# Attention stage: side work between uses, value and output tiles by twos in a bank, projections copied once, turned maxima copied by VectorE

## The reference

```
qkv = layernorm(x) @ Wqkv + bqkv              # 16 heads of 16 channels
scores = q k^T / 4 - slope[h] * |i - j|       # 1024 x 1024 for each batch element and head
out = softmax(scores) @ v                     # over all 1024 keys, no causal mask
x = x + out @ Wout + bout
```

## Time and profile before

| | us |
|---|---|
| median of 3 runs (3257.17 to 3265.41) | 3258.13 |
| the profiled execution, own time | 3271.27 |
| its span in the trace | 3269.5 |
| first to last score matmul of attention (L1742) | 1248.7 to 2917.9 |
| PE, DVE, ACT, POOL busy over the span | 94%, 78%, 61%, 33% |

### The profile page before, as it was taken

How to read it: one execution, slowest core, us unless ns; L and a number is a source line. 1 busy time by engine, 2 the same in 40 slices (tenths; PEclk the granted TensorE clock), 3 DMA queues, 4 the chain that set the end, 5 groups by cost and what they waited for, 6 DMA issues and landing times. The chain is left out here.

```text
span 3269.5 us, 73440 instructions
## 1 busy us (share of the span) xinstructions
PE 3085.7 (94%) x28196; PEld 1827.7 (56%) x28196; DVE 2534.6 (78%) x5875; ACT 1985.8 (61%) x2967; POOL 1094.2 (33%) x1364
## 2 busy tenths in 40 slices
PE   7999999995999869999999999999999999988999
PEld 3666666664788734444454444444544445437888
DVE  6677877764788658888888889788888887927887
ACT  2455444441666515777777777767777777775665
POOL 3354554443223221332423333323233232222222
PEclk8899999985999958999999999999999999998999
DMA  1000000002111151324232323232322322202111
GB/s 54 2 28 28 28 28 28 20 10 73 66 59 59 39 108 36 58 39 83 40 67 55 57 63 60 43 77 52 71 48 49 74 49 53 57 18 93 52 60 38
DMA packets 126461, 165.34 MB, mean 51 GB/s; under 512 B 23584, under 2 KB 104240, under 8 KB 125456
## 3 DMA queue, kind: packets, MB, share of 16 engines
q1 hardware_dynamic: 115688, 149.37, 18.7%
q0 software_dynamic: 9984, 10.38, 2.4%
q10 hardware_dynamic: 440, 0.90, 0.1%
HBM read 81.58 MB, written 38.24 MB: 37 GB/s over the span
## 5 line engine op out<-in xcount | busy, mean ns | idle before, releaser
L1855 ACT ACTIVATE b_p_t<-banks 128x1024 f32<-128x1024 f32 x1024 | 1040.2, 1027 | 304.0 <-PE banks L1742 238.7
L1681 PE MATMUL banks<-b_k_stack,b_q_stack 62*128 62x512 f32 x2048 | 809.6, 475 | 26.5 <-issue 10.8
L1742 PE MATMUL banks<-b_q_stack,b_k_stack 64*128 64x512 f32 x2048 | 767.8, 450 | 9.9 <-ACT b_p_t L1855 9.9
L1941 DVE CUSTOM_DVE_ANT_1 banks<-banks,b_near_rows 128x512 f32<-128x512 f32 x960 | 649.0, 715 | 138.3 <-PE banks L1681 135.1
L1944 DVE TENSOR_REDUCE b_half_max<-banks 128x1 f32<-128x512 f32 x1024 | 657.8, 684 | 79.9 <-PE banks L1681 76.3
L1696 PE MATMUL banks<-b_p_t,b_v 128*17 128x256 f32 x8192 | 631.8, 386 | 6.3 <-POOL b_p_t L2100 5.5
L1742 PEld LDWEIGHTS banks<-b_q_stack,b_k_stack 64*128 64x128 f32 x2048 | 313.7, 185 | 389.1 <-issue 325.5
L2100 POOL TENSOR_TENSOR b_p_t<-b_p_t,b_fall 128x256 f32<-128x256 f32 x384 | 280.5, 733 | 658.6 <-ACT b_p_t L1855 657.8
L1681 PEld LDWEIGHTS banks<-b_k_stack,b_q_stack 62*128 62x128 f32 x2048 | 341.9, 188 | 111.6 <-DVE b_half_max L1941 35.9
L1696 PEld LDWEIGHTS banks<-b_p_t,b_v 128*17 128x17 f32 x8192 | 142.8, 95 | 300.7 <-issue 162.2
L1148 ACT ACTIVATE ffn_relu<-banks,ffn_scale_fc 128x512 f32<-128x512 f32 x256 | 176.2, 688 | 205.5 <-PE banks L1080 205.5
(11 more groups left out here) (255 smaller groups left out, 5333.6 us busy)
## 6 DMA issues: line engine op xcount, KB each, us to landing
ffn_x<-x SPq DMA_DIRECT2D x32, 512.0 KB, 3.9
b_q_stack<-b_qk_hi SPq DMA_DIRECT2D x252, 64.0 KB
b_k_stack<-b_qk_hi SPq DMA_DIRECT2D x252, 64.0 KB
b_fall<-c_fall SPq DMA_DIRECT2D x48, 256.0 KB, 2.6
a_x<-hidden_states SPq DMA_DIRECT2D x16, 512.0 KB, 3.9
x<-a_x SPq DMA_DIRECT2D x16, 512.0 KB, 2.9
x<-ffn_x SPq DMA_DIRECT2D x16, 512.0 KB, 2.8
b_x<-x SPq DMA_DIRECT2D x8, 1024.0 KB, 5.6
```

Source lines behind the costliest of these rows:

```text
L1681: pe.matmul(m, q_stack[rows, slot, qb * P:(qb + 1) * P], k_stack[rows, slot, half * BANK:(half + 1) * BANK], start=True, stop=True, tile_p ...
L1742: last = pe.matmul(out, k_stack[stack, slot, kb * P:(kb + 1) * P], q_stack[stack, slot, half * BANK:(half + 1) * BANK], start=True, stop=n ...
L1855: act.activation(p_t[use % P_BUFS][:, :, :], scores[use % 2], ACT.Exp, scale=slopes()[pair][0]).then_inc(p_made, 1)
L1941: dve.tensor_tensor_reduce(out=m, in0=m, in1=near_window(pair, qb, rg), scale=1.0, scalar=LOWEST, op0=ALU.add, op1=ALU.max, accum_out=larg ...
```

## The change

- The merge goes by whole uses: `attend` yields once a use instead of twice, so that side work no longer stands between the two halves of one.
- Stacks count eight steps instead of two of weight three, and the halves are made in steps 2 and 3 of them; SP's DMAs stay behind three such steps. ACT copies a half once, as `qk`, and POOL rounds that to `qk_hi` itself before it makes `qk_lo`.
- Value and output tiles go by twos in a bank: one copy of 128x512 where there were two of 128x256. `att_hi`, `att_lo` and `y` have one buffer for two tiles in place of two buffers for one, and the first output step only turns.
- The turned maxima come two maxima later (`TURN` 4) and behind the use's matmuls, and DVE copies them.

```diff
-        STEPS, STACKS, VALUES, NORMALIZE = GROUP * HALVES * QB, 2, QB, 1 + QB
+        STEPS, STACKS, VALUES, NORMALIZE = GROUP * HALVES * QB, 8, QB // 2, 1 + QB
+        STACK_STEPS = {2: 0, 3: 1}
-        LEAD, TURN = 16, 2
+        LEAD, TURN = 16, 4
...
-                side_by_side(*([(STEPS, attend(g, rows), 1)] if g >= 0 else []),
+                side_by_side(*([(STEPS // ROWGROUPS, attend(g, rows), 1)] if g >= 0 else []),
...
-                             *([(STACKS, stacks(g + 2), 3)] if 0 <= g + 2 < ALL else []),
+                             *([(STACKS, stacks(g + 2), 1)] if 0 <= g + 2 < ALL else []),
...
# PE, find_maxima
-                    if g and turn == TURN:
-                        m, (used, n) = misc.take(("turn", g - 1), (shift_copied, g))
...
                         yield
+                    if g and turn == TURN - 1:
+                        m, (used, n) = misc.take(("turn", g - 1), (shift_copied, g))
...
# ACT, make_stacks
-                    act.activation(qk_hi[:, cols], m, ACT.Identity, bias=b_scaled[:, hg:hg + 1],
-                                   scale=scale_qk[:, 0:1]).then_inc(qk_hi_made, 1)
...
# POOL, make_stacks
+                        pool.tensor_copy(qk_hi[:, cols], qk[:, cols]).then_inc(qk_hi_made, 1)
+                        pool.wait_ge(qk_hi_made, use + 1)
                         pool.tensor_tensor(qk_lo[:, cols], qk[:, cols], qk_hi[:, cols].bitcast(F32), ALU.subtract).then_inc(qk_lo_made, 1)
...
# ACT, find_maxima, and DVE, find_maxima
-                        act.activation(shift_full[:, :], m, ACT.Copy, scale=-1.0).then_inc(shift_copied, 1)
+                    if g and turn == TURN:
+                        dve.wait_ge(max_turned, g)
...
+                        dve.tensor_scalar(shift_full[:, :], misc.at["turn", g - 1][0:2 * GROUP * QB, 0:P], -1.0, None, ALU.mult).then_inc(shift_copied, 1)
...
# SP, make_stacks
-                yield
-                yield
+                for _ in range(max(STACK_STEPS)):
+                    yield
                 sp.wait_ge(bias_cast, 16)
                 sp.wait_ge(qk_hi_made, 2 * (g + 1))
                 sp.wait_ge(qk_lo_made, 2 * (g + 1))
```

More of the change, by code:

```diff
@@ L1657, in make_stacks @@
                 pe.wait_ge(x_lo_made, 4 * (b + 1))
-                for half in range(HALVES):
+                for step in range(STACKS):
+                    if step not in STACK_STEPS:
+                        yield
+                        continue
+                    half = STACK_STEPS[step]
                     cols = slice(half * BANK, (half + 1) * BANK)
@@ L1713, in conclude @@
                 pe.wait_ge(att_made, use + 1)
[L1714 to L1717, removed]
+                for n in range(TWOS + 1):
+                    tiles = TWOS * b + n
+                    if n:
+                        m, (used, value) = misc.take(("y", b, n - 1), (y_made, tiles))
+                        pe.wait_ge(used, value)
+                        pe.wait_ge(att_lo_made, tiles)
+                        if tiles == 1:
+                            pe.wait_ge(weights_split, 3)
+                        for j in range(2):
+                            tokens = slice(j * P, (j + 1) * P)
+                            last = in_three(m[:, j * DIM:(j + 1) * DIM], lambda part, kt: (att_hi, att_lo)[part][:, kt, tokens],
+                                            lambda part, kt: w_out[part][:, kt, :])
+                        last.then_inc(y_ready, 1)
+                    if n < TWOS:
+                        m, (used, value) = misc.take(("att", b, n), (att_lo_made, tiles + 1))
+                        pe.wait_ge(used, value)
                         for kt in range(KT):
-                            last = pe.transpose(m[:, kt * P:(kt + 1) * P], att[:, i, kt * P:(kt + 1) * P], ident[:, :])
+                            for j in range(2):
+                                last = pe.transpose(m[:, (kt * 2 + j) * P:(kt * 2 + j + 1) * P], att[:, 2 * n + j, kt * P:(kt + 1) * P], ident[:, :])
                         last.then_inc(att_turned, 1)
[L1721 to L1729, removed]
                     yield
@@ L1828, in conclude @@
                     return
[L1829 to L1843, removed]
+                for n in range(TWOS + 1):
+                    tiles = TWOS * b + n
+                    if n:
+                        act.wait_ge(y_ready, tiles)
+                        if tiles >= 2:
+                            act.wait_ge(y_added, tiles - 1)
+                        act.activation(y[:, :, :], misc.at["y", b, n - 1].rearrange("p (t n) -> p t n", t=2), ACT.Copy).then_inc(y_made, 1)
+                    if n < TWOS:
+                        act.wait_ge(att_turned, tiles + 1)
+                        if tiles:
+                            act.wait_ge(y_ready, tiles)
+                        act.activation(att_hi[:, :, :], misc.at["att", b, n].rearrange("p (k n) -> p k n", k=KT), ACT.Copy).then_inc(att_hi_made, 1)
                     yield
@@ L1966, in conclude @@
                     return
[L1967 to L1976, removed]
+                for n in range(TWOS + 1):
+                    tiles = TWOS * b + n
+                    if n < TWOS:
+                        dve.wait_ge(att_hi_made, tiles + 1)
+                        if tiles:
+                            dve.wait_ge(y_ready, tiles)
+                        dve.tensor_tensor(att_lo[:, :, :], misc.at["att", b, n].rearrange("p (k n) -> p k n", k=KT),
+                                          att_hi[:, :, :].bitcast(F32), ALU.subtract).then_inc(att_lo_made, 1)
                     yield
@@ L2084, in conclude @@
                     return
-                for i in range(QB):
-                    x, tile = xs[b % X_BUFS][:, i, :], QB * b + i
-                    pool.wait_ge(y_made, tile + 1)
-                    pool.wait_ge(x_biased, tile + 1)
-                    pool.tensor_tensor(x, x, y[tile % 2][:, :], ALU.add).then_inc(y_added, 1)
+                for n in range(TWOS + 1):
+                    if n:
+                        x, tiles = xs[b % X_BUFS][:, 2 * n - 2:2 * n, :], TWOS * b + n
+                        pool.wait_ge(y_made, tiles)
+                        pool.wait_ge(x_biased, 2 * tiles)
+                        pool.tensor_tensor(x, x, y[:, :, :], ALU.add).then_inc(y_added, 1)
                     yield
```

134 lines of the change are left out of this document (71 added, 63 removed).

## The result

The changed kernel takes 3422.18 us (median of 4 runs, 3409.19 to 3429.16) against 3257.65 for the kernel before on the same chip (4 runs, 3252.87 to 3265.41): ratio 1.0498, 95% interval 1.0460 to 1.0536, 164 us slower. Forecast were 120 slower, 3378, with a range of 3300 to 3440.

A forecast was written before the change was run, and what follows sets the result against it. PE's program, with DVE close behind, was taken to set attention's pace. Stack waits of 156 us, less 73 of gains, plus 4 at the tail and 33 of clock, gave +120: 3378 us from 3258, range 3300 to 3440.

The forecast's parts named there:

- wait for head 2: PE waits at use 24 for head 2's stacks: 5.9 us in `hg` 0 and 2, 4.4 in 1 and 3; 156 us.
- row of maxima: The maxima's DMA on SP lands by the group's end: counted 0, with up to 0.8 us a group against it.
- clock: PE's granted clock falls behind each stack wait: 30 groups at 1.1 us, 33 us lost (0 to 71).
- gains in attention: Turned maxima, halves, output and values save 3.4, 1.0, 2.0 and 3.2 us in `hg` 0 to 3; 73 us over the stage.
- The chain to head 2: From the second half's first matmul through SP's DMAs to head 2 in place: 20.7 us (20.0 to 21.7).
- PE's side: PE's own work from the second half to use 24: 14.8 us in `hg` 0 and 2, 16.3 in 1 and 3.
- SP is not moved past other queues: SP keeps its order, stacks behind the `fall` load and maxima's DMA behind the stacks; 0 us counted for the row of maxima.
- the smaller of my two prices: Lower-clock `hg` 1 groups took 1.1 or 2.4 us more; 1.1 was taken for each group's wait, 33 us over 30.
- The output's 1.4: Output tiles by pairs in `hg` 0: 0.2 us a pair from a saved switch, 0.6 from the first step; 1.4 us gained.
- Rival 1: Stacks at use 24 come in time and the gains stand: 69 us faster, 3189 us; chance 0.08.
- Rivals 2 and 4: Stack chain of 18.5 us, 40 slower, 3300, chance 0.10; or of 17.5, gains and waits cancelling, chance 0.04.
- Rival 3: Clock stays low longer, 2.4 us a wait, and the row of maxima 0.8 late: 183 slower, 3441 us; chance 0.10.

The follow-up runs named there:

- e1_early: The changed kernel with its halves behind uses 2 and 6 in place of 10 and 14, SP's place for the stacks unchanged: 3223.95 us.
- e6_order_store: e3_head_order with the output's store and next element's load issued behind the maxima's DMAs in `hg` 0, in place of ahead of them: 3302.21 us.
- e3_head_order: The changed kernel with SP issuing a group's stack DMAs for heads 0, 2, 1, 3 in place of 0, 1, 2, 3: 3330.75 us.
- e9_early_turn2: e1_early with the maxima turned one pair earlier (`TURN` 2), behind the first pair, still copied by DVE: 3219.18 us.
- e10_early_singles: e1_early with value and output tiles one to a bank and two buffers each, as in the kernel before: 3219.34 us.

## Why the prediction was right, and where it was off

The direction, the mechanism and the place were right: the earlier trace rows held a margin of 2 us, and the half moved by six uses. Term by term, from the traces of the profiled executions:

| term | forecast | measured |
|---|---|---|
| wait for head 2 | +156 | +124.0 |
| row of maxima | 0 | +26.9 |
| clock | +33 | some +48, a remainder, with the refill of the engines |
| gains in attention | -73 | some -50 |
| tail | +4 | +5 |

The clock's is what is left between the changed kernel and e1_early over the 30 groups: 1743.8 - 1555.8 = 188, less 124 and less 16 of row waits. The gains are the 40 us by which e1_early's groups are shorter than before, and the 10 it still waits for the row. These terms add up to 154 us, for 120 forecast; the medians are 164 apart.

- **The chain to head 2** was forecast at 20.7 and took 19.3: 4.65 to SP's first DMA (4.9; POOL's rounding is 0.61 where I took 0.8), 20 steps of issue in 12.36, not 13.7, and 2.27 from there to PE's start, for 2.1. **PE's side** was right, 14.85 for 14.8 (the terms given for it add up to 14.7); with `hg` 3 and 1, at some 16.0 and 16.8, close to the 16.3 too. The waits are 4.8 us in `hg` 0 and 4.9 in `hg` 2 (5.9), 3.2 and 3.7 in `hg` 1 and 3 (4.4).
- **The step that failed** is "SP is not moved past other queues", with 0 for the row of maxima, which measured 26.9. In `hg` 0 (15.4 us) the order on SP's queue is the same, but the stacks' delay pushed the store and the load into the maxima's time, and there a DMA of 32 KB behind a load of 1 MB took 5.4 us to the next issue, 2.6 in e6_order_store, where no load stood ahead. e3_head_order shows that this was the next deadline, hardly later than the first: mending the first alone gave nothing back in the six inner `hg` 0 groups. In `hg` 2 (9.4 us) it is the other half of that passage: the later turn was seen to bring the row "close to the group's end" and counted 0, up to 0.8 a group against it, and it cost 1.0 to 1.4; with `TURN` 2 in e9_early_turn2 these waits are all but gone.
- **The clock.** It was under 1.00 in nearly every group, as said, and the 48 us are 1.6 a wait for the 1.1 taken. The rule of the Trainium skill (TensorE: Matmul & The Clock Gate, section HAM oscillation), half of the throttled time, gave 50 on a group at 0.97; the 30 groups had 0.94 against 0.99 in e1_early, by which it would be 0.06 x 1744 - 0.01 x 1556 = 89 us, an estimate that the rounding of the two shares moves by up to 16. What is left for the clock here is about half of that. By this remainder, which no run separated, the rule is too dear for this kernel, and the smaller of my two prices was too cheap.
- **The gains** were over-counted by a third. By e1_early: 1.25 us in `hg` 0 (forecast 3.4), 0.5 in `hg` 1 (1.0), 0.8 in `hg` 2 (2.0), 2.8 in `hg` 3 (3.2). The kernel before does not repeat itself in `hg` 1, where single groups with a lower clock took up to 56.2 us: against its undisturbed 53.8, e1_early's 54.1 are a loss of 0.3. The output's 1.4 were the worst: e10_early_singles has its pairs at a loss of 0.61, and whether their single buffers make it was not tested. Uses 25 and 26 took 3.43 us in e1_early's plain group, where 2.84 was said, for 3.88 before.
- **The rivals.** Rival 1's 3189 is what e1_early would have been with the forecast gains; it was 3224. Rivals 2 and 4 needed a shorter chain, and 19.3 was not short enough. Rival 3 had the signs right for both of its terms, clock and row, but the waits and the gains came out smaller. Its 3441 is nearer to the 3422 than the forecast's 3378, whose own range, up to 3420, was passed by 2 us. That the sum erred by only 44 us owes something to luck, since the errors had both signs: the stacks' waits were put 32 too high, the row 27 and the clock 15 too low, and the gains 23 too high.
- **What was to be seen:** the waits, the first SP DMA, the low clock and ACT's missing `shift_full` (now 273 ns on DVE) are there. The plain groups took 51.2 to 53.7 us, three of seven within the 50 to 52, and of uses 25 and 26 only the second takes 1.23.

## What to carry to other kernels

Where one queue issues a chain of many small DMAs, write its start, pace and every deadline behind it on one line before moving what starts it; a margin of 2 us is a limit. When a wait is mended, look for the next consumer of the same queue first: here stacks, maxima and the next input fell due one after the other, and only moving the start mended all three. Price parts of a change singly where they can be: the single copy, the turn and the pairs of values gained, the pairs of output lost, and the two times, before and after, showed none of it.

## What the runs showed of the hardware

A small DMA issued behind a large one pays for it: 32 KB from issue to the next dependent issue took 1.81 us alone in a plain group (2097.76 to 2099.57), 2.58 in `hg` 0 with no load ahead (1937.98 to 1940.56, e6_order_store) and 5.4 there, 0.49 us behind a 1 MB load (1982.97 to 1988.36). SP's issues of the stack DMAs, six of 64 KB within SBUF and one of 56 KB from DRAM for a head, follow each other at 0.62 us here (20 steps in 12.36), at 0.68 in the group of the earlier trace rows. POOL rounds 128x512 in 0.61 us, half of the 1.28 of its two-input difference in that shape. The granted clock of code that no edit touched differed from one execution to the next, 0.88 and 1.00 over the same 100 us, and attention began 16 us earlier: two profiled executions are not to be subtracted as a whole.
